# Taps loaded as rows and turned on TensorE, the routing token turned earlier, and the first norm's epsilon and mean handled by GpSimd

## The chip, the cores and the metric

The kernel runs on one core of a Trainium2 chip. The metric is the device time in microseconds of one execution. Engines are named as in the profile: PE is TensorE, PEld its loads of the stationary operand, DVE VectorE, ACT ScalarE, POOL GpSimd, SP the engine that issues most DMAs.

## The reference

One pre-norm block on x of shape (8, 1024, 256), all float32:

```
x = x + mixer(layernorm(x));  x = x + experts(layernorm(x))
layernorm: (x - mean) / sqrt(var + 1e-5), over the 256 features
mixer: xp, z = split(x @ w_in)                     # 256 -> 512 + 512
       xc = silu(causal_conv(xp, conv_w) + conv_b) # 4 taps per channel, depthwise
       h[t] = 0.9 h[t-1] + 0.1 (xc[t] @ w_B)       # 512 -> 16
       y = (h @ w_C) * silu(z);  return y @ w_out  # 512 -> 256
experts: scores = x[:, 0, :] @ Wr + br             # first token of each sequence
       top 2 of 8; mean over them of gelu(x @ W1[e] + b1[e]) @ W2[e] + b2[e]
```

## The kernel before

The 8192 tokens are worked in 16 chunks of 512 (TT = 4 tiles of 128 tokens), two chunks a sequence. Chunk a is in the mixer, chunk a - 1 in the output projection and second norm, chunk a - 2 in the experts, all in one step. The first three chunks are written out by hand in `opening()` of every engine, one more step follows, then a hardware loop and a written-out end. Each engine has its own program (sync, gpsimd, scalar, vector, tensor blocks) and runs it strictly in order; semaphores with counts tie them together. There is no planner: the order in each `opening()` and `step()` is the schedule.

Every product is made of three TensorE passes over operands split into a high and a low part (`_hi`, `_lo`): hi by hi, lo by hi, hi by lo. ScalarE casts the high part; VectorE or GpSimd subtracts it from the value for the low part. Normed tokens must be turned (tokens on partitions to features on partitions); for chunks 0 to 3 TensorE does it (`turns`), later the data go through DRAM and VectorE.

What the change touches:
- Opening loads. SP issues the first half of chunk 0, `w_in` in three parts, chunk 1, eight copies of `w_C`, `w_out` and the rest. ScalarE's queue carries the second half of chunk 0, the taps `tap_w` (L583, runs of 16 bytes), `tap_b` (L585, 4 bytes each) and `wb_raw` (L586).
- First norm of chunk 0 in halves of two tiles. VectorE makes the moments (`stats1_first`: L883, L888), the negated mean (L892) and variance plus epsilon (L893); GpSimd the power -1/2 (L480); VectorE the normed tiles (`norm1_first`, L900). TensorE turns each half (`turns1_first`, L1218) behind WARM = 32 turns of the identity (L1466), ScalarE casts it, and `xp_first` (L1290, L1293, L1301) makes the first products.
- First norm of the other chunks. VectorE: `stats1`, `moments1` (L848, then L851 negates the means and L852 adds epsilon). GpSimd: `pow1` (L395) and `norm1` (L408, adds the negated mean and multiplies).
- Taps. ScalarE does tap 0 with the bias (`first_taps`, L651), VectorE the other three (`tap`, L958), reading one column of `tap_w` per block.
- Second norm and routing of chunk 0. ScalarE: `norm2(0, 0)`, four tiles (L634), then `first_token(0)`, `state_hi(1, 1)`, `gates(2, 2)`. TensorE: `z(2, (0, 1, 2))`, then `turns2_first`: tile 0 (L1241), the token's two turns into `blk[0]` (L1247), the other tiles, `score(0, 0)` (L1459), and `z(2, (3,))`. VectorE: `route(0)` picks the experts, then `state_lo(1, 1)`, a tap, `ys(1, (0,))`, `turn2_lo(0)`. TensorE's `up_first` (L1349, L1353, L1357) starts the experts of chunk 0.

## Time and profile before

| | us |
|---|---|
| median of 3 runs | 510.37 (510.25 to 510.47) |
| the profiled execution, its own time | 510.43 |
| its span in the profile | 508.5 |
| TensorE busy | 503.3 |
| VectorE busy | 453.2 |
| ScalarE busy | 401.0 |
| GpSimd busy | 343.1 |

A timeline row gives the start from the beginning of the span, the time from the first start to the last end of the merged instructions, the engine, the source line, the operation, what is written and read, the count, and in brackets the idle time before it with what ended it. TensorE's instructions are pipelined: each is shown longer than its turn on the array, so the distance between starts is what it costs, and the last of a group ends later than its turn. A row with four products of 512 columns and 1.07 us holds three distances of 0.227 and one product of 0.39.

### The profile page before, as it was taken

Reading aid. Unit: us, or ns where it says so; the run is one execution under the profiler, and the core shown is the slowest. Engines: PE = TensorE matmul, PEld = TensorE weight load, DVE = VectorE, ACT = ScalarE, POOL = GpSimd, SP = SyncE. Lnnn points to the kernel's source line nnn. Section 1 sums busy time; section 2 is a strip of 40 time slices with the busy share of each in tenths; the row PEclk is TensorE's granted clock in tenths of the full one; section 3 lists DMA queues with packets and bytes.
Section 4 is the critical chain, followed back from the end, with each engine's and each line's share of the span. In section 5 each row is a group of like instructions: output and inputs, shape, how many; then the busy total and the mean of one; then the engine's idle time right before and its main releaser. Section 6 shows DMA issues by size and latency. Waiting matters only on the chain.

```text
span 508.5 us, 9829 instructions
## 1 busy us (share of the span) xinstructions
PE 503.3 (99%) x3026; PEld 447.5 (88%) x3026; DVE 453.2 (89%) x900; ACT 401.0 (79%) x694; POOL 343.1 (67%) x384
## 2 busy tenths in 40 slices
PE   8999999999999999999999999999999999999997
PEld 8878799889898989989899998989989899898997
DVE  6999999999998899979999899998999889896773
ACT  4886958888869789697886969879797888969454
POOL 4866587649694696928969197772977649773291
PEclk9999999999999999999999999999999999999999
DMA  8940104435151542606235171542604333130102
GB/s 263 291 177 1 42 1 167 124 125 167 62 175 56 156 132 83 206 0 206 83 124 165 41 217 30 165 124 78 211 31 147 111 124 126 50 116 0 43 2 83
DMA packets 53378, 57.27 MB, mean 113 GB/s; under 512 B 8682, under 2 KB 49642, under 8 KB 53226
## 3 DMA queue, kind: packets, MB, share of 16 engines
q1 hardware_dynamic: 51498, 56.67, 34.8%
q10 hardware_dynamic: 1856, 0.31, 0.3%
q8 instruction: 12, 0.20, 0.2%
q14 instruction: 12, 0.10, 0.1%
HBM read 35.46 MB, written 21.50 MB: 112 GB/s over the span
## 4 chain that ended last, share of the span: by engine, by line
PE 93%; DVE 1%; POOL 0%; issue 0%; DVEq 0%
PE blk L1257 15%; PE blk L1258 15%; PE blk L1262 15%; PE tok L1374 12%; PE tok L1376 12%; PE tok L1375 12%; PE turn L1415 3%; PE turn L1418 3%; PE blk L1437 3%; PE turn L1209 1%; POOL normed L408 0%; PE tok L1262 0%; PE tok L1257 0%; PE tok L1258 0%; PE turn L1258 0%; PE turn L1257 0%
## 5 line engine op out<-in xcount | busy, mean ns | idle before, releaser
L958 DVE SCALAR_TENSOR_TENSOR conv<-blk,tap_w,conv 128x512 f32<-128x512 f32 x192 | 130.1, 742 | 7.8 <-ACT conv L651 7.1
L462 POOL TENSOR_TENSOR y_lo<-gate,y_hi 128x512 fp32r<-128x512 f32 x57 | 72.2, 1297 | 36.6 <-ACT y_hi L580 36.6
L1257 PE MATMUL blk<-xn_hi,w_in_hi 128*128 128x512 f32 x228 | 89.5, 393 | 0.0
L1258 PE MATMUL blk<-xn_hi,w_in_lo 128*128 128x512 f32 x228 | 89.0, 391 | 0.0
L427 POOL TENSOR_TENSOR xc_lo<-conv,xc_hi 128x512 fp32r<-128x512 f32 x59 | 70.9, 1218 | 8.8 <-ACT xc_hi L580 8.0
L1374 PE MATMUL tok<-w_out_hi,y_hi 128*128 128x256 f32 x256 | 72.1, 282 | 0.0
L1376 PE MATMUL tok<-w_out_hi,y_lo 128*128 128x256 f32 x256 | 71.8, 281 | 0.0
L1375 PE MATMUL tok<-w_out_lo,y_hi 128*128 128x256 f32 x256 | 71.8, 281 | 0.0
L1262 PE MATMUL blk<-xn_lo,w_in_hi 128*128 128x512 f32 x228 | 70.3, 389 | 0.0
L1374 PE MATMUL tok<-w_hi,hid_hi 128*128 128x256 f32 x248 | 69.9, 282 | 0.0
L1376 PE MATMUL tok<-w_hi,hid_lo 128*128 128x256 f32 x248 | 69.6, 281 | 0.0
L1375 PE MATMUL tok<-w_lo,hid_hi 128*128 128x256 f32 x248 | 69.5, 280 | 0.0
L651 ACT ACTIVATE conv<-blk,tap_b,tap_w 128x512 f32<-128x512 f32 x64 | 48.9, 777 | 25.0 <-PE blk L1262 22.4
L657 ACT ACTIVATE conv<-conv 128x512 f32<-128x512 f32 x64 | 39.3, 629 | 31.3 <-DVE conv L958 30.3
L829 DVE TENSOR_TENSOR hid_lo<-hid,hid_hi 128x512 fp32r<-128x512 f32 x64 | 45.4, 736 | 17.6 <-ACT hid_hi L580 17.3
L470 POOL TENSOR_TENSOR x_mid<-x_mid,b_sel 128x256 f32<-128x256 f32 x60 | 45.7, 794 | 12.9 <-ACT normed L634 7.9
L1262 PEld LDWEIGHTS blk<-xn_lo,w_in_hi 128*128 128x128 f32 x228 | 42.8, 188 | 9.2
L1258 PEld LDWEIGHTS blk<-xn_hi,w_in_lo 128*128 128x128 f32 x228 | 42.9, 188 | 8.0
L1257 PEld LDWEIGHTS blk<-xn_hi,w_in_hi 128*128 128x128 f32 x228 | 42.8, 188 | 8.0
L1375 PEld LDWEIGHTS tok<-w_out_lo,y_hi 128*128 128x128 f32 x256 | 49.0, 191 | 0.6
L1374 PEld LDWEIGHTS tok<-w_out_hi,y_hi 128*128 128x128 f32 x256 | 48.0, 188 | 0.8
L1375 PEld LDWEIGHTS tok<-w_lo,hid_hi 128*128 128x128 f32 x248 | 47.4, 191 | 1.1
(185 smaller groups left out, 1320.9 us busy)
## 6 DMA issues: line engine op xcount, KB each, us to landing
spill<-normed SPq DMA_DIRECT2D x25, 512.0 KB, 2.8
normed<-spill SPq DMA_DIRECT2D x100, 128.0 KB, 2.9
out<-x_mid SPq DMA_DIRECT2D x30, 256.0 KB, 2.8
x_mid<-in_L_attn_x SPq DMA_DIRECT2D x29, 256.0 KB, 2.8
x_in<-in_L_attn_x SPq DMA_DIRECT2D x14, 512.0 KB, 4.6
w_all<-in_L_ffn_W SPq DMA_DIRECT2D x2, 2048.0 KB, 11.6
b_all<-in_L_ffn_b SPq DMA_DIRECT2D x1, 1024.0 KB, 13.1
gate<-in_L_attn_w_in SPq DMA_DIRECT2D x2, 256.0 KB, 4.7
```

Of the source, the lines that this page charges most:

```text
L427: nc.gpsimd.tensor_tensor(xc_lo[:, j, :], conv[:, j, 0:CH], xc_hi[:, j, :].bitcast(F32), ALU.subtract).then_inc(xc_lo_set, 1)
L462: nc.gpsimd.tensor_tensor(y_lo[:, j, :], gate_of(o, j), y_hi[:, j, :].bitcast(F32), ALU.subtract).then_inc(y_lo_set, 1)
L470: ins = nc.gpsimd.tensor_tensor(mid(f, q)[:, n, :], mid(f, q)[:, n, :], b2_sel[:], ALU.add)
L651: nc.scalar.activation(conv[:, j, HALO:HALO + CH], blk[j][:], ACT.Identity, bias=tap_b[:, j:j + 1], scale=tap_w[:, j, 0:1]).then_inc(tap_f ...
L829: return nc.vector.tensor_tensor(dst, src, hi.bitcast(F32), ALU.subtract)
L958: nc.vector.scalar_tensor_tensor(cols, blk[j][:], tap_w[:, j, t:t + 1], cols, ALU.mult, ALU.add).then_inc(tap_added, 1)
L1257: mm(dst, whi(k), his(k), start=(k == 0), stop=False)
L1258: mm(dst, wlo(k), his(k), start=False, stop=False)
L1262: ins = mm(dst, whi(k), los(k), start=False, stop=(k == KD - 1))
L1374: mm(dst, his[:, j, rows], whi, start=(j == 0 and n == 0), stop=False, skip_group_check=True)
L1375: mm(dst, his[:, j, rows], wlo, start=False, stop=False, skip_group_check=True)
L1376: ins = mm(dst, los[:, j, rows], whi, start=False, stop=(last and n == 1), skip_group_check=True)
```

## The change

The convolution's taps and bias are loaded as rows: channel block j on partition j, 2 KB and 512 bytes contiguous. Behind the 26th of the 32 warm-up turns TensorE waits for them and turns each tap and the bias (five turns of 4 by 128) into a bank; VectorE copies the 20 columns to `taps_all`. `wb_raw` moves from ScalarE's queue to SP's, ahead of the copies of `w_C`.

The first norm no longer has a negated mean: the mean is subtracted. In chunk 0 the fourth tile is centred and scaled by ScalarE between its casts of `w_in` instead of by VectorE, TensorE waiting for it before that tile's turn and GpSimd before its first low part. In the other chunks VectorE only makes the moments; GpSimd adds epsilon, waits for itself, and takes the power.

The routing token is turned on TensorE behind `z(2, (0, 1))`, in front of `z(2, (2,))`; ScalarE casts it between the second and third tile of `norm2(0, 0)`; the score is issued behind tile 1 instead of behind tile 3; `gates(2, 2)` goes ahead of `state_hi(1, 1)`.

```diff
@@ -46,8 +46,9 @@
-        tap_w = sb("tap_w", [P, JD, TAPS])
-        tap_b = sb("tap_b", [P, JD])
+        taps_all = sb("taps_all", [P, TAPS + 1, JD])
+        tap_b = taps_all[:, TAPS, :]
+        tap_rows = sb("tap_rows", [JD, (TAPS + 1) * P])
         w_router, w_spread = sb("w_router", [P, KD, E]), sb("w_spread", [P, KD, E])
@@ -289,6 +292,7 @@
                 sp.dma_start(x_mid[:, 1, half_rows(h), :], x_t[1][:, half_rows(h), :]).then_inc(res_loaded[1][h], 16)
+            sp.dma_start(wb_raw[:], w_B.rearrange("(j p) s -> p j s", p=P)).then_inc(mix_loaded, 16)
             for r in range(P // NST):
@@ -392,6 +396,10 @@
                 pool.wait_ge(stats1_ready, c + 1)
+                pool.sem_inc(passed, 1)
+                nc.gpsimd.tensor_scalar(var_eps1[:], mean_var1[:, :, 1], EPS, None, ALU.add).then_inc(eps_added, 1)
+                pool.wait_ge(eps_added, c)
+                pool.sem_inc(passed, 1)
                 nc.gpsimd.tensor_tensor(rstd1[:], var_eps1[:], minus_half[:], ALU.pow).then_inc(rstd1_set, 1)
@@ -405,7 +413,7 @@
                         dst, src = by_group(normed1, n), src.rearrange("p (k g j) -> p k g j", k=KD, g=QUADS)
-                    ins = nc.gpsimd.tensor_scalar(dst, src, neg_mean[:, n:n + 1], rstd1[:, n:n + 1], ALU.add, ALU.mult)
+                    ins = nc.gpsimd.tensor_scalar(dst, src, mean_var1[:, n, 0:1], rstd1[:, n:n + 1], ALU.subtract, ALU.mult)
                 ins.then_inc(norm1_ready, 1)
@@ -480,6 +488,7 @@
                 pool.wait_ge(norm1_ready, 1)
+                pool.wait_ge(tile_normed, 1)
                 for part in (1, 2):
@@ -580,10 +589,8 @@
             act.dma_start(x_mid[:, 0, half_rows(1), :], x_t[0][:, half_rows(1), :]).then_inc(res_loaded[0][1], 16)
-            act.dma_start(tap_w[:], conv_w.rearrange("(j p) o t -> p j (o t)", p=P)).then_inc(taps_loaded, 16)
-            with nc.allow_non_contiguous_dma(reason="a small transposed load, once"):
-                act.dma_start(tap_b[:], conv_b.rearrange("(j p) -> p j", p=P)).then_inc(taps_loaded, 16)
-            act.dma_start(wb_raw[:], w_B.rearrange("(j p) s -> p j s", p=P)).then_inc(mix_loaded, 16)
+            act.dma_start(tap_rows[:, 0:TAPS * P], conv_w.rearrange("(j p) o t -> j (p o t)", p=P)).then_inc(taps_loaded, 16)
+            act.dma_start(tap_rows[:, TAPS * P:], conv_b.rearrange("(j p) -> j p", p=P)).then_inc(taps_loaded, 16)
             act.wait_ge(consts_set, 1)
@@ -609,6 +616,19 @@
+            def centre_tile():
+                act.wait_ge(stats1_ready, 1)
+                hi(neg_mean[:], mean_var1[:, TT - 1, 0:1], -1.0).then_inc(mean_negated, 1)
+                act.wait_ge(mean_negated, 1)
+                nc.scalar.activation(by_token(normed1, TT - 1), tokens_in(0)[:, TT - 1, :], ACT.Identity,
+                                     bias=neg_mean[:]).then_inc(tile_centred, 1)
+
+            def scale_tile():
+                act.wait_ge(tile_centred, 1)
+                act.wait_ge(rstd1_set, 1)
+                nc.scalar.activation(by_token(normed1, TT - 1), by_token(normed1, TT - 1), ACT.Copy,
+                                     scale=rstd1[:, TT - 1:TT]).then_inc(tile_normed, 1)
+
             def turn1_hi_first(h):
@@ -709,11 +729,13 @@
                 in_hi(0)
+                centre_tile()
                 in_hi(1)
+                scale_tile()
                 turn1_hi_first(0)
...
                 in_hi(2)
-                act.wait_ge(taps_loaded, 32)
+                act.wait_ge(taps_set, 1)
                 first_taps(0, (0, 1))
@@ -758,10 +780,11 @@
                 gates(2, 0)
-                norm2(0, 0)
+                norm2(0, 0, (0, 1))
                 first_token(0)
+                norm2(0, 0, (2, 3))
+                gates(2, 2)
                 state_hi(1, 1)
-                gates(2, 2)
                 gates(2, 1)
@@ -842,14 +865,13 @@
                 dve.wait_ge(norm1_ready, c)
-                dve.wait_ge(stat1_step, c * 2 + 3)
+                if isinstance(c, int) and c == 1:
+                    dve.wait_ge(tile_normed, 1)
+                dve.wait_ge(stat1_step, c + 4)
                 dve.sem_inc(passed, 1)
...
                     ins = nc.vector.bn_aggr(mean_var1[:, n, :], stats1_t[:, n, :])
-                ins.then_inc(stat1_step, 1)
-                dve.wait_ge(stat1_step, c * 2 + 4)
-                nc.vector.tensor_scalar(neg_mean[:], mean_var1[:, :, 0], -1.0, None, ALU.mult)
-                nc.vector.tensor_scalar(var_eps1[:], mean_var1[:, :, 1], EPS, None, ALU.add).then_inc(stats1_ready, 1)
+                ins.then_inc(stats1_ready, 1)
@@ -889,16 +911,15 @@
                 cols = half_rows(h)
-                nc.vector.tensor_scalar(neg_mean[:, cols], mean_var1[:, cols, 0], -1.0, None, ALU.mult)
                 nc.vector.tensor_scalar(var_eps1[:, cols], mean_var1[:, cols, 1], EPS, None,
...
                 dve.sem_inc(passed, 1)
-                for n in (2 * h, 2 * h + 1):
-                    ins = nc.vector.tensor_scalar(by_token(normed1, n), tokens_in(0)[:, n, :], neg_mean[:, n:n + 1],
-                                                  rstd1[:, n:n + 1], ALU.add, ALU.mult)
+                for n in (2 * h, 2 * h + 1)[:2 - h]:
+                    ins = nc.vector.tensor_scalar(by_token(normed1, n), tokens_in(0)[:, n, :], mean_var1[:, n, 0:1],
+                                                  rstd1[:, n:n + 1], ALU.subtract, ALU.mult)
                 ins.then_inc(norm1_ready if h else half_normed, 1)
@@ -1047,9 +1068,12 @@
                 in_lo_first(1)
+                dve.wait_ge(taps_turned, 1)
+                nc.vector.tensor_copy(taps_all[:].rearrange("p t j -> p (t j)"),
+                                      tok[1][:, 0:(TAPS + 1) * JD]).then_inc(taps_set, 1)
                 turn1_lo_first(0)
                 turn1_lo_first(1)
-                dve.wait_ge(taps_loaded, 32)
+                dve.wait_ge(taps_set, 1)
                 edge(0, True)
@@ -1210,11 +1234,21 @@
+            def turn_taps():
+                pe.wait_ge(taps_loaded, 32)
+                by_tap = tap_rows[:, 0:TAPS * P].rearrange("j (p t) -> j t p", t=TAPS)
+                for t in range(TAPS + 1):
+                    src = by_tap[:, t, :] if t < TAPS else tap_rows[:, TAPS * P:]
+                    ins = nc.tensor.transpose(tok[1][:, t * JD:(t + 1) * JD], src, ident[0:JD, 0:JD])
+                ins.then_inc(taps_turned, 1)
+
             def turns1_first():
...
                         for t in (2 * h, 2 * h + 1):
+                            if t == TT - 1 and k == 0:
+                                pe.wait_ge(tile_normed, 1)
                             ins = nc.tensor.transpose(half_bank(h, k)[:, t * P:(t + 1) * P],
@@ -1231,10 +1265,16 @@
+            def token_first():
+                pe.wait_ge(tap_added, last_tap(2, 0))
+                pe.wait_ge(norm2_ready, 1)
+                for k in range(KD):
+                    nc.tensor.transpose(blk[0][:, k * P:(k + 1) * P], by_token(normed2, 0)[:, k * P:(k + 1) * P],
+                                        ident[:]).then_inc(token_turned, 1)
+
             def turns2_first():
...
                 pe.wait_ge(gate_set, 2 * JD + 1)
-                pe.wait_ge(tap_added, last_tap(2, 0))
                 for t in range(TT):
@@ -1242,11 +1282,8 @@
                             ins.then_inc(turned2, 1)
-                    if t == 0:
-                        for k in range(KD):
-                            nc.tensor.transpose(blk[0][:, k * P:(k + 1) * P], by_token(normed2, 0)[:, k * P:(k + 1) * P],
-                                                ident[:]).then_inc(token_turned, 1)
-                score(0, 0)
+                    if t == 1:
+                        score(0, 0)
@@ -1462,7 +1499,9 @@
                 pe.wait_ge(consts_set, 3)
-                for _ in range(WARM):
+                for n in range(WARM):
+                    if n == WARM - 6:
+                        turn_taps()
                     nc.tensor.transpose(tok[0][:, 0:P], ident[:], ident[:])
@@ -1489,7 +1528,9 @@
                 state_in(1)
-                z(2, (0, 1, 2))
+                z(2, (0, 1))
+                token_first()
+                z(2, (2,))
                 turns2_first()
```

## Rows read from the trace of the kernel before

**Rows 1.** The page's busy times over the whole span.
```profile
PE 503.3 (99%) x3026; PEld 447.5 (88%) x3026; DVE 453.2 (89%) x900; ACT 401.0 (79%) x694; POOL 343.1 (67%) x384
```

**Rows 2.** TensorE's waits from 8 us on: total us, times, longest.
```profile
PE tok L1257 <- ACT gate L669: 0.5, 1, 0.5
PE turn L1209 <- POOL normed L408: 0.3, 1, 0.3
```

**Rows 3.** Windows: stretch, its length, busy us (x instructions) by engine, clock, DMA, GB/s.
```profile
60.00:500.00 440.00, 440.00 (x2673) 392.75 (x2673) 396.82 (x768) 354.55 (x608) 303.58 (x336) 1.00 0.33 107
```

**Rows 4.** TensorE's timeline, opening: start, us, line, out<-in, count, [idle before].
```profile
1.84 5.33 PE L1466 MATMUL tok<-ident 128*128 128x128 f32 x24
...
7.17 0.88 PE L1466 MATMUL tok<-ident 128*128 128x128 f32 x6
...
7.88 0.60 PE L1218 MATMUL blk<-ident,normed 128*128 128x128 f32 x4
8.58 0.66 PE L1218 MATMUL turn<-ident,normed 128*128 128x128 f32 x4
```

**Rows 5.** DMA issues: queue, count, KB each, us from issue to landing.
```profile
x_mid<-in_L_attn_x ACTq DMA_DIRECT2D x1, 256.0 KB, 3.6
...
tap_b<-in_L_attn_conv_b ACTq DMA_DIRECT2D x1, 2.0 KB, 6.8
```

**Rows 6.** VectorE's timeline, 6 to 25 us.
```profile
6.67 0.74 DVE L900 TENSOR_SCALAR normed<-x_mid,neg_mean,rstd 128x256 f32<-128x256 f32 x2
...
7.79 0.74 DVE L900 TENSOR_SCALAR normed<-x_mid,neg_mean,rstd 128x256 f32<-128x256 f32 x2
...
12.25 0.91 DVE L851 TENSOR_SCALAR neg_mean<-mean_var 128x4 f32<-128x4 f32 x1
...
13.15 6.67 DVE L958 SCALAR_TENSOR_TENSOR conv<-blk,tap_w,conv 128x512 f32<-128x512 f32 x10
...
24.51 0.17 DVE L851 TENSOR_SCALAR neg_mean<-mean_var 128x4 f32<-128x4 f32 x1
```

**Rows 7.** ScalarE's timeline, 6 to 13 us.
```profile
6.95 0.63 ACT L580 ACTIVATE w_in_hi<-gate 128x512 fp32r<-128x512 f32 x1 [0.79 <-DMA gate<-in_L_attn_w_in]
...
8.30 0.66 ACT L580 ACTIVATE xn_hi<-blk 128x256 fp32r<-128x256 f32 x2 [0.72 <-PE blk L1218]
...
11.75 1.45 ACT L651 ACTIVATE conv<-blk,tap_b,tap_w 128x512 f32<-128x512 f32 x2 [1.09 <-PE blk L1301]
```

**Rows 8.** GpSimd's timeline, 10 to 52 us.
```profile
10.73 2.41 POOL L474 TENSOR_TENSOR w_in_lo<-gate,w_in_hi 128x1024 fp32r<-128x1024 f32 x1 [0.73 <-ACT w_in_hi L580]
...
24.83 1.46 POOL L395 TENSOR_TENSOR rstd<-var_eps,minus_half 128x4 f32<-128x4 f32 x1 [1.81 <-DVE var_eps L852]
26.49 2.16 POOL L408 TENSOR_SCALAR normed<-x_in,neg_mean,rstd 128x256 f32<-128x256 f32 x4 [0.20 <-issue]
...
51.08 0.20 POOL L422 TENSOR_TENSOR shift<-neg_mean,rstd 128x4 f32<-128x4 f32 x1 [0.18 <-POOL rstd L419]
```

**Rows 9.** TensorE's timeline, 27 to 60 us.
```profile
27.38 1.07 PE L1418 MATMUL tok<-xc_lo,b_mix 128*128 128x512 f32 x4
...
28.71 1.09 PE L1209 MATMUL turn<-ident,normed 128*128 128x128 f32 x8 [0.26 <-POOL normed L408]
...
51.82 0.39 PE L1257 MATMUL tok<-xn_hi,w_in_hi 128*128 128x512 f32 x1
...
54.37 0.24 PE L1459 MATMUL blk<-w_router,first_tok 128*1 128x8 f32 x4
55.12 0.50 PE L1257 MATMUL tok<-xn_hi,w_in_hi 128*128 128x512 f32 x1 [0.50 <-ACT gate L669]
...
58.49 1.49 PE L1353 MATMUL blk<-xn_lo,w_hi 128*128 128x512 f32 x4
```

**Rows 10.** ScalarE's timeline at the second norm of chunk 0.
```profile
51.31 2.09 ACT L634 ACTIVATE normed<-x_mid,shift,rstd 128x256 f32<-128x256 f32 x4
```

**Rows 11.** VectorE's timeline behind the routing.
```profile
57.69 1.28 DVE L829 TENSOR_TENSOR xn_lo<-turn,xn_hi 128x512 fp32r<-128x512 f32 x2
```

More of the change, by code:

```diff
@@ L61, in build_block @@
         rstd1, rstd2 = sb("rstd1", [P, TT]), sb("rstd2", [P, TT])
-        neg_mean = sb("neg_mean", [P, TT])
+        neg_mean = sb("neg_mean", [P, 1])
         neg_mean2, shift2 = sb("neg_mean2", [P, TT]), sb("shift2", [P, TT])
@@ L109, in build_block @@
         wout_loaded = sem("wout_loaded")
[L110 removed]
+        taps_loaded, taps_turned, taps_set = sem("taps_loaded"), sem("taps_turned"), sem("taps_set")
         mix_loaded = sem("mix_loaded")
@@ L977, in edge @@
                 if opens:
-                    src = tap_b[:].rearrange("p (j o) -> p j o", o=1).broadcast_to([P, JD, HALO])
+                    src = tap_b.rearrange("p (j o) -> p j o", o=1).broadcast_to([P, JD, HALO])
                 else:
```

7 lines of the change are left out of this document (4 added, 3 removed).

## The prediction

> **What bounds the kernel now.** I read the page's busy times first: TensorE is busy 99% of the span [rows 1]. Then its waits: in the whole span it waits for other engines twice after its start, 0.3 and 0.5 us [rows 2]. The windows show it busy 440.00 of the 440 us from 60 to 500 [rows 3]. So nothing that the change does in the steady steps can pay; an edit pays only where it closes a hole in TensorE's row before 60 us, and hurts where it opens one or adds TensorE work. The timeline shows four holes. (a) Between the two halves of the first turns: four turns start at 7.88, at 0.11 us a piece they are through at 8.32, and the next four start at 8.58 [rows 4]: 0.26 of idle, and 0.06 more because the first turn behind a pause takes 0.17 instead of 0.11. (b) Before turns1(2) at 28.71: the last of the four products that start at 27.38, 0.227 apart, leaves the array at 28.29, so 0.42 plus 0.06 of restart [rows 9]. (c) Between the score (four steps, the last starting at 54.45) and z(2,3) at 55.12, 0.64 and 0.11 of restart. (d) Inside L1353: four products take 1.49, where four together take 1.07 (0.39 for the last, 0.227 for the others): 0.42 [rows 9]. Together 1.97 us, 0.39% of the time: about the most that can be won.
>
> **The opening: what it removes.** Each half of the first statistics drops one neg_mean operation on VectorE, about 0.08 of its time (two such operations of 0.17 overlap in the 0.32 between 24.51 and the pow at 24.83 [rows 6, 8]); the second half's var_eps is thus 0.16 sooner. norm1_first(1) norms one tile instead of two: it began at 7.79 and took 0.74 for two [rows 6], so it now ends near 8.00 (7.79 - 0.16 + 0.38). The other tile is ScalarE's: negate (about 0.2), centre (0.38, half of a 512-wide copy's 0.63 [rows 7] with its fixed part) from about 6.65, then in_hi(1), which started at 6.95 and now waits till about 7.3, takes 0.63, then scale 0.38: ready at about 8.3. The second half's turns could start at 8.1 instead of 8.58.
>
> **The opening: what it adds.** TensorE works in order, and the 32 warm-up turns, not the data, set the first turns: 24 of them run from 1.84 for 5.33, 0.213 a piece, the six from 7.17 take 0.88, 0.11 a piece but for the first (the clock rises from 1.2 to 2.4 GHz there), and the first half's normed tiles are ready at 7.41 (6.67 + 0.74), before 7.88 [rows 4, 6]. The five tap turns are inserted behind the 26th, at 7.17. No row shows a turn with a 128-column stationary operand and 4 moving columns. Lower bound 0.025 (the score's steps, 0.24 for four with 0.17 for the last, one stationary column [rows 9]): 0.13 in all. Upper bound: full turns at the low clock, 0.213: 1.07. Nearest is a full turn at 2.4 GHz, 0.11, with the same stationary operand but 32 times the moving columns; I take 0.08, 0.40 in all. First turns then start at 8.28, the second four follow at once at 8.72 (tiles ready at 8.3), and are through at 9.16, where they were at 9.07 (8.58 + 0.17 + three of 0.11): hole (a) of 0.31 is used up and **+0.1** is left (bounds -0.2 and +0.8). ScalarE's first cast follows the turns (it began at 8.30 behind 7.88 [rows 7]), so it begins at about 8.7 and ends at 9.08, just before TensorE wants it; the second operand is wanted at 9.4 and there at 9.36. This cover is thin: 0.05.
> The Trainium skill (TensorE: Matmul & The Clock Gate, LDWEIGHTS) says that a weight load costs by its columns and not by its rows, so that loading 4 rows by 128 columns costs what 128 by 128 does; by its formula, an estimate, 0.107 a load, 0.53 for five, and the sum below would end at 509.9. No row here separates the load from the moving part.
>
> The loads: taps as rows are 4 runs of 2 KB and 4 of 512 B, where 512 and 512 tiny ones went. tap_b landed 6.8 us after its issue at about 1.8, the 256 KB of x_mid ahead of it on the same queue 3.6 after its issue at 0.7 [rows 5]. So the new ones land after 4.3 and, if they cost no more than the old, by 8.6. I take 5: TensorE reaches them at 7.17, so they are hidden by 2 us. wb_raw goes behind six issues on SP's queue; every later issue (eight of w_C, w_out, x_in, the router, the experts' weights) is about 0.5 later. Their first reader is ScalarE after 13.1, at the end of the two products' taps that begin at 11.75 [rows 7]; a delay of a few tenths there meets taps that VectorE reaches only at 16.5. Cost 0, up to 0.1.
>
> **VectorE and the first hole in the steps.** L851 at 12.25 took 0.91 and ended with GpSimd's L474 (10.73 plus 2.41 is 13.14), where one of its size takes 0.17 [rows 6, 8]: it was held by GpSimd. It goes, and VectorE's first tap, 13.15 before, waits only for ScalarE's first taps, 11.75 plus 0.78, and the second for 13.2. From the third tap on VectorE is about 0.6 ahead; with the opening's 0.1, 0.5. The new copy of the taps out of PSUM, 0.17, falls at 8.5 to 8.7 before a wait for ScalarE. If GpSimd holds it as it held L851, it ends near 9.7, and the 0.5 is lost.
> moments1(2) loses two operations: the moments were done at 24.51, where the first of them starts, and the pow started at 24.83 [rows 6, 8], of which I take 0.25 as won. GpSimd adds epsilon: a small operation of 0.20 and 0.18 of waiting for its own result, as before L422 [rows 8]. So its pow starts 0.5 + 0.25 - 0.38 = 0.37 earlier than 24.83, and the four norm tiles, 26.49 to 28.66, end at 28.3, or sooner if the pow's 1.46 [rows 8] was stretched by VectorE's work beside it. TensorE arrives at 28.29 + 0.1. Hole (b) closes: **-0.48**. If VectorE's 0.5 is lost, GpSimd is 0.13 late and the hole grows by 0.1: bounds -0.48 and +0.1.
> What comes after moves with TensorE: turn casts, scan, gates, y_lo are released by it or by VectorE, which has gained as much.
>
> **The routing token.** ScalarE's four norm2 tiles start at 51.31, 0.50 apart and 0.6 long [rows 10], so tile 0 is ready at 51.95; TensorE ends z(2,1) at 51.82 [rows 9]: the token's turns wait, 0.13 plus 0.06. z(2,2) then runs from 52.25 to 53.6, with the token's two one-column casts at 52.45, two tiles of norm2 behind it until 53.65. Turns of tiles 0 and 1, then the score's last step at 54.23, where it was at 54.45. Tiles 2 and 3 turn by 54.7, the gate that z(2,3) wants (gates(2,2), now ahead of state_hi) is done at 54.35: z(2,3) starts at 54.7 instead of 55.12, hole (c) closed but for the new 0.2. Yet that is not what comes last: VectorE's route, state_lo, tap and turn2_lo follow the score. turn2_lo(0), 57.69 and 1.28 long [rows 11], releases the second product of L1353. This chain moves by 0.22, so of (c) 0.22 is kept and TensorE waits longer in (d) and for state_lo. **-0.22** (bounds 0 and -0.45). w1 is cast 0.1 to 0.16 sooner, and GpSimd's w_lo behind it is due 0.5 later.
>
> **Steady steps.** GpSimd gets 0.38 more in each of 13 chunks, VectorE loses 0.16 to 1.0. TensorE never waits there [rows 3]: 0.
>
> **The sum**: +0.1 - 0.48 - 0.22 = -0.6. Against the profiled execution (span 508.5, 1.93 around it, 510.43) 509.83; that is 0.06 above the median of the runs, so 509.77.
>
> **Rivals.** (1) The opening eats it: the tap turns run near the low clock's 0.213 each, or the copy is held by GpSimd. Then +0.5 to +0.8, hole (b) closes partly, route kept: +0.6 - 0.48 - 0.22 = -0.1, 510.27. For it: they start at the very turn of the clock. Against: the row of six. (2) More: tap turns at 0.03, so -0.2, and the route's chain shorter, -0.45: 509.25. For it: the score's steps; against: turn2_lo is a fixed chain. (3) Slower: the wait on the tap load stands in front of the last warm-up turns, and in front of the first half of the tokens. If the load lands after 7.17, TensorE stands and every tenth is paid in full; at the old landing of tap_b, 8.6, that is +1.4, and if the clock, whose rise at 7.2 came after 5.6 us of unbroken turns, stays at 1.2 GHz through as long again, half of it, 2.8, comes on top. It decides from a landing at 7.17; net of the other -0.6 that is +0.8 (511.2) without the clock and +3.6 (514.0) with it; I name the middle, 512.6. Against: the load lies behind only 256 KB that landed at 4.3. (4) The change does not do what it says, the old holes reopening one engine further on: 510.4.
> In a sentence of its own: the Trainium skill (TensorE: Matmul & The Clock Gate, Part 4: PE-mode transpose) says that transposes do not count as work that lifts the clock; here the rise came behind 26 of them and nothing else [rows 4], so this trace disagrees, and inserted turns should neither help nor hinder it.
>
> **Chances.** Forecast 0.56 (509.77, its own range 509.4 to 510.1); (1) 0.16; (2) 0.10; (3) 0.08; (4) 0.10. 0.2%, 1.02 us, is about what a measurement can tell from no change. Faster by more (under 509.35) is (2) and a corner of the forecast: 0.13. Slower (over 511.39) is (3): 0.07. The rest 0.80. Range 509.1 to 510.8: it takes in (1), (4) and most of (2), and leaves out (3).
>
> **What would show it.** Tap turns: five short TensorE rows at 7.17, and the first turns about 0.4 after 7.88; no pause between the two halves. L851 gone and the first VectorE tap near 12.6. No TensorE wait on GpSimd's normed near 28. The score near 0.2 sooner relative to turns1(2), no wait for a gate, but waits on state_mix and xn_lo. TensorE's span from there to the end unchanged behind L1353 (508.5 - 58.5 = 450.0). A tap load landing after 7.2, or a TensorE wait in the steady steps, would make the forecast wrong.

## The result, and the profile after

The changed kernel takes 532.63 us (median of 4 runs, 528.16 to 535.02) against 510.34 for the kernel before in the same comparison: 1.0427 times as long, interval 1.0400 to 1.0454. The prediction was 509.77. The profiled execution took 533.95, span 532.0.

The page's busy times (as [rows 1]) show TensorE busy 10.1 us longer and the span longer by 23.5, so 13.4 of it is new idle time. The 10.1 are no new work: about 5 are three stretches at the lower of TensorE's two clocks (1.7 us each, see the end), and the rest, an estimate from the distances between its starts, is delays too short for the page to show as idle. GpSimd is busy 52.7 us more and VectorE 20.1:

```profile
PE 513.4 (96%) x3031; PEld 450.6 (85%) x3031; DVE 473.3 (89%) x868; ACT 404.7 (76%) x697; POOL 395.8 (74%) x399
```

The costliest groups after: line, engine, operation, busy time and mean ns.

```profile
L416 POOL TENSOR_SCALAR normed<-x_in,mean_var,rstd 128x256 f32<-128x256 f32 x56 | 67.9, 1225 | 2.8 <-POOL rstd L403 2.0
...
L852 DVE TENSOR_TENSOR xn_lo<-normed,xn_hi 128x512 fp32r<-128x512 f32 x50 | 65.8, 1356 | 1.4 <-ACT xn_hi L589 0.7
```

GpSimd's norm tile, the line that only swapped `add` of the negated mean for `subtract` of the mean, takes 1225 ns; four of the old ones together took 2.16 in [rows 8]. Sixty tiles (56 here, four of chunk 1) by 0.67 are 40 of GpSimd's 52.7. The group of VectorE's low parts of the normed tiles has grown too, by 21.8, though the change doesn't touch it. This is how the same group stood before:

```profile
L829 DVE TENSOR_TENSOR xn_lo<-normed,xn_hi 128x512 fp32r<-128x512 f32 x50 | 44.0, 919 | 1.4 <-ACT xn_hi L580 0.7
```

TensorE's waits after (as [rows 2]; the wait for ident is its start, as before):

```profile
PE turn L1455 <- POOL xc_lo L435: 4.6, 3, 2.0
PE blk L1299 <- DVE xn_lo L852: 4.4, 4, 2.5
PE turn L1233 <- POOL normed L416: 2.2, 1, 2.2
PE tok L1411 <- DVE hid_lo L852: 1.7, 3, 0.6
PE tok L1505 <- POOL ident L393: 1.6, 1, 1.6
PE blk L1474 <- DVE state_mix L852: 0.7, 3, 0.3
PE blk L1394 <- POOL w_lo L445: 0.3, 1, 0.3
```

Behind the start 7.1 us of them are waits for GpSimd and 6.8 waits for VectorE's low parts.

The windows (as [rows 3]) show the two places where the time goes, the opening, and the steady steps, where TensorE had been busy 440.00 of 440:

```profile
12.00:20.00 8.00, 6.15 (x30) 4.85 (x28) 7.36 (x15) 6.64 (x14) 7.53 (x7) 1.00 0.71 184
20.00:28.00 8.00, 7.63 (x31) 6.27 (x32) 5.51 (x15) 6.03 (x11) 7.58 (x11) 0.79 1.08 383
...
60.00:500.00 440.00, 427.98 (x2531) 375.80 (x2530) 406.53 (x717) 347.00 (x593) 338.22 (x334) 0.99 0.33 106
```

GpSimd's timeline of the opening gives the first of them, chunk 1's norm; the row below it is that norm in the kernel before:

```profile
13.80 0.24 POOL L400 TENSOR_SCALAR var_eps<-mean_var 128x4 f32<-128x4 f32 x1
14.23 1.04 POOL L403 TENSOR_TENSOR rstd<-var_eps,minus_half 128x4 f32<-128x4 f32 x1 [0.18 <-POOL var_eps L400]
15.48 4.84 POOL L416 TENSOR_SCALAR normed<-x_mid,mean_var,rstd 128x256 f32<-128x256 f32 x4 [0.21 <-issue]
```

```profile
14.54 2.17 POOL L408 TENSOR_SCALAR normed<-x_mid,neg_mean,rstd 128x256 f32<-128x256 f32 x4 [0.22 <-issue]
```

It takes 4.84 for four tiles, and TensorE, which turned them at 17.41 before, stands until 20.37. Behind that pause the granted clock is 0.79 of full in 20 to 28 us: products of 512 columns then start 0.43 apart until 24.7; they start 0.23 apart before the pause and again from 25. TensorE's timeline:

```profile
17.54 0.61 PE L1299 MATMUL tok<-xn_lo,w_in_hi 128*128 128x512 f32 x2
20.37 1.09 PE L1233 MATMUL turn<-ident,normed 128*128 128x128 f32 x8 [2.22 <-POOL normed L416]
...
22.12 0.63 PE L1294 MATMUL tok<-xn_hi,w_in_hi 128*128 128x512 f32 x1
22.54 0.63 PE L1295 MATMUL tok<-xn_hi,w_in_lo 128*128 128x512 f32 x1
```

In the steady steps the largest single loss is a VectorE low part. Its timeline and GpSimd's, at 159 to 167 us:

```profile
159.31 1.28 DVE L881 TENSOR_TENSOR x_mid<-tok,x_mid 128x512 f32<-128x512 f32 x2
160.62 7.24 DVE L852 TENSOR_TENSOR xn_lo<-normed,xn_hi 128x512 fp32r<-128x512 f32 x2
...
159.31 2.36 POOL L435 TENSOR_TENSOR xc_lo<-conv,xc_hi 128x512 fp32r<-128x512 f32 x2
161.61 2.83 POOL L478 TENSOR_TENSOR x_mid<-x_mid,b_sel 128x256 f32<-128x256 f32 x4
164.40 2.31 POOL L435 TENSOR_TENSOR xc_lo<-conv,xc_hi 128x512 fp32r<-128x512 f32 x2
```

Two low parts take 7.24 where they take 1.3 undisturbed; the first alone has 6.64. GpSimd runs without a break to 166.71, and the first low part ends 0.55 behind that: it was held while GpSimd's train (its operations one behind the other, without a pause) passed, and then did its own work. TensorE waits 2.5 us for it, and again the clock falls, to a mean of 0.57 in the 4 us behind the wait:

```profile
168.00:172.00 4.00, 4.00 (x11) 3.13 (x12) 3.67 (x19) 2.13 (x4) 1.23 (x2) 0.57 0.00 0
```

### The profile page after: what moved, and what is told of

Same layout as the page of the kernel before. It is cut to its first block, busy times and chain, and to the rows that moved or that the text cites. A ratio compares the mean times of both kernels' runs of the same rounds, so it can differ in the third digit from the quotient of the medians.

```text
span 532.0 us, 9853 instructions
## 1 busy us (share of the span) xinstructions
PE 513.4 (96%) x3031; PEld 450.6 (85%) x3031; DVE 473.3 (89%) x868; ACT 404.7 (76%) x697; POOL 395.8 (74%) x399
## 4 chain that ended last, share of the span: by engine, by line
PE 62%; DVE 10%; POOL 10%; issue 8%; ACT 3%; ACTq 1%; DVEq 0%; POOLq 0%
PE blk L1294 10%; PE blk L1299 10%; PE blk L1295 9%; PE tok L1411 8%; PE tok L1413 8%; PE tok L1412 8%; POOL xc_lo L435 3%; PE blk L1474 3%; DVE xn_lo L852 2%; DVE conv L979 2%; POOL w_lo L445 2%; POOL normed L416 2%; PE turn L1455 2%; DVE hid_lo L852 2%; PE turn L1452 2%
## 5 line engine op out<-in xcount | busy, mean ns | idle before, releaser
L979 DVE SCALAR_TENSOR_TENSOR conv<-blk,taps_all,conv 128x512 f32<-128x512 f32 x192 | 130.2, 741 | 8.9 <-ACT conv L671 7.8
L435 POOL TENSOR_TENSOR xc_lo<-conv,xc_hi 128x512 fp32r<-128x512 f32 x59 | 73.2, 1257 | 5.6 <-ACT xc_hi L589 5.5
L1411 PE MATMUL tok<-w_hi,hid_hi 128*128 128x256 f32 x248 | 71.0, 286 | 1.7 <-DVE hid_lo L852 1.7
L416 POOL TENSOR_SCALAR normed<-x_in,mean_var,rstd 128x256 f32<-128x256 f32 x56 | 67.9, 1225 | 2.8 <-POOL rstd L403 2.0
L671 ACT ACTIVATE conv<-blk,taps_all 128x512 f32<-128x512 f32 x64 | 49.4, 778 | 26.9 <-PE blk L1299 24.5
L852 DVE TENSOR_TENSOR xn_lo<-normed,xn_hi 128x512 fp32r<-128x512 f32 x50 | 65.8, 1356 | 1.4 <-ACT xn_hi L589 0.7
L852 DVE TENSOR_TENSOR hid_lo<-hid,hid_hi 128x512 fp32r<-128x512 f32 x64 | 47.9, 786 | 11.2 <-ACT hid_hi L589 10.8
L478 POOL TENSOR_TENSOR x_mid<-x_mid,b_sel 128x256 f32<-128x256 f32 x60 | 51.4, 887 | 4.8 <-DVE hid_lo L852 4.1
L716 ACT ACTIVATE hid<-blk,b_sel 128x512 f32<-128x512 f32 x64 | 43.3, 677 | 11.2 <-PE blk L1299 9.0
L1411 PEld LDWEIGHTS tok<-w_hi,hid_hi 128*128 128x128 f32 x248 | 47.4, 191 | 4.0 <-DVE hid_lo L852 3.0
```

What stands on the lines that cost most here:

```text
L416: ins = nc.gpsimd.tensor_scalar(dst, src, mean_var1[:, n, 0:1], rstd1[:, n:n + 1], ALU.subtract, ALU.mult)
L435: nc.gpsimd.tensor_tensor(xc_lo[:, j, :], conv[:, j, 0:CH], xc_hi[:, j, :].bitcast(F32), ALU.subtract).then_inc(xc_lo_set, 1)
L478: ins = nc.gpsimd.tensor_tensor(mid(f, q)[:, n, :], mid(f, q)[:, n, :], b2_sel[:], ALU.add)
L852: return nc.vector.tensor_tensor(dst, src, hi.bitcast(F32), ALU.subtract)
L979: nc.vector.scalar_tensor_tensor(cols, blk[j][:], taps_all[:, t, j:j + 1], cols, ALU.mult, ALU.add).then_inc(tap_added, 1)
L1411: mm(dst, his[:, j, rows], whi, start=(j == 0 and n == 0), stop=False, skip_group_check=True)
```

## The experiments

Two theories stood at first. A: GpSimd's `subtract, mult` form is itself slow. B: the tile is slow because of its operands or of what runs beside it.

**e1.** Seven forms of GpSimd's 128x256 operation on one core with nothing beside them, six of each; the rest of the block is left out.

```diff
+    forms = [(ALU.add, ALU.mult), (ALU.subtract, ALU.mult), (ALU.mult, ALU.add), (ALU.mult, ALU.subtract),
+             (ALU.add, None), (ALU.subtract, None), (ALU.mult, None)]
```

> A kernel that leaves the whole block out and only runs GpSimd tensor_scalar on one 128x256 tile, six times in each of seven forms of its two operations. Theory A (the operation: GpSimd is slow at subtract followed by mult): the form subtract, mult takes about 1.22 us as in the changed kernel, add, mult 0.556 as in the one before, the others tell whether subtract or its place is slow. Theory B (the operand: a mean read with a step of two, or VectorE beside it): all forms take about 0.55 us here.

The groups, in the order resb `subtract, mult`, resd `mult, subtract`, rese to resg one operation alone (add, mult, subtract, each 924), resc `mult, add`, resa `add, mult`:

```profile
L57 POOL TENSOR_SCALAR resb<-src,mv 128x256 f32<-128x256 f32 x6 | 7.3, 1223 | 0.6
L57 POOL TENSOR_SCALAR resd<-src,mv 128x256 f32<-128x256 f32 x6 | 7.3, 1222 | 0.6
...
L55 POOL TENSOR_SCALAR resg<-src,mv 128x256 f32<-128x256 f32 x6 | 5.5, 924 | 0.6
...
L57 POOL TENSOR_SCALAR resc<-src,mv 128x256 f32<-128x256 f32 x6 | 3.3, 557 | 0.6
L57 POOL TENSOR_SCALAR resa<-src,mv 128x256 f32<-128x256 f32 x6 | 3.3, 554 | 2.7 <-DMA src<-in_L_attn_x 2.2
```

A is shown: two scalars with add and mult in either order take 0.555; one subtract among them makes it 1.22, and a single operation, add too, takes 0.92, more than two. B falls.

**e2.** The kernel before with that form alone.

```diff
-ins = nc.gpsimd.tensor_scalar(dst, src, neg_mean[:, n:n + 1], rstd1[:, n:n + 1], ALU.add, ALU.mult)
+ins = nc.gpsimd.tensor_scalar(dst, src, mean_var1[:, n, 0:1], rstd1[:, n:n + 1], ALU.subtract, ALU.mult)
```

> The kernel before with one line changed: GpSimd's norm1 subtracts the mean from mean_var1 instead of adding neg_mean; everything else stays, the negated mean is still made. If that line is the cause of the loss (theory A or B), 60 tiles go from 0.556 to 1.22 us and the time is 528 to 535. Rival C (the cause is GpSimd's added epsilon and its wait, or the new chunk-0 code): the time stays at 510.3.

544.66 (542.27 to 548.89), ratio 1.0678 (1.0618 to 1.0738): the form alone costs more than the whole change, and more than I expected. Its main waits were VectorE's:

```profile
PE blk L1262 <- DVE xn_lo L829: 10.7, 10, 2.0
PE tok L1374 <- DVE hid_lo L829: 7.5, 6, 1.7
PE turn L1209 <- POOL normed L408: 3.8, 2, 1.9
```

Ten of its low parts are held for 2.8 to 6.1 us; in the changed kernel it is four, for 3.3 to 6.6.

**e3.** The changed kernel with `add` for `subtract`; it computes x plus the mean.

```diff
-ins = nc.gpsimd.tensor_scalar(dst, src, mean_var1[:, n, 0:1], rstd1[:, n:n + 1], ALU.subtract, ALU.mult)
+ins = nc.gpsimd.tensor_scalar(dst, src, mean_var1[:, n, 0:1], rstd1[:, n:n + 1], ALU.add, ALU.mult)
```

> The changed kernel with add in the place of subtract in GpSimd's norm1, the operand still mean_var1 (it computes x + mean, so it leaves the right value out). Theory A (operation): 0.556 a tile, TensorE without waits in the steady steps, 509.5 to 510.3. Theory B (operand with step two): 1.22 a tile, 528 to 535 as the changed kernel.

509.94 (509.33 to 510.66), ratio 0.9988 (0.9978 to 0.9997); after its start TensorE waits once, 0.4. The tile takes 0.555 though it reads the same operand. One word in one line carries all of the 22 us, and everything else of the change together brings 0.5 (before took 510.42 in this comparison), which is what the prediction said of it (0.6).

**e4.** The repair that keeps VectorE out: GpSimd negates the mean itself in one more small operation and uses `add, mult`.

```diff
+nc.gpsimd.tensor_scalar(neg_means[:], mean_var1[:, :, 0], -1.0, None, ALU.mult).then_inc(eps_added, 1)
...
-ins = nc.gpsimd.tensor_scalar(dst, src, mean_var1[:, n, 0:1], rstd1[:, n:n + 1], ALU.subtract, ALU.mult)
+ins = nc.gpsimd.tensor_scalar(dst, src, neg_means[:, n:n + 1], rstd1[:, n:n + 1], ALU.add, ALU.mult)
```

> The changed kernel with a negated mean made by GpSimd (one more operation of 0.23 us on 128x4 per chunk) and add, mult in norm1. Theory A and B: 0.556 a tile again, steady steps without TensorE waits, and the time is what the rest of the change is worth: 509.8 by the old sum with the measured tap turns put in (five steps of 0.12 instead of 0.08, so +0.2 more: 510.0). If a part of the loss lies elsewhere, it stays above 511.

515.78 (515.00 to 516.29), ratio 1.0100 (1.0084 to 1.0117): my expectation missed by 5.8. The fast form is back, and 0.2 more a chunk on GpSimd than in e3 still costs 5.8 us. TensorE waits nowhere longer than 0.2; the time is in the distances between its starts. Behind the five held low parts ten of them are 0.17 to 0.38 longer than usual, 2.8 together, and six at `state_mix` are 0.2 to 0.3 longer, 1.5 together. VectorE's low parts take 1304 on the mean, five of them 4.2. GpSimd and VectorE at one of the five:

```profile
214.57 2.83 POOL L480 TENSOR_TENSOR x_mid<-x_mid,b_sel 128x256 f32<-128x256 f32 x4
217.35 2.34 POOL L437 TENSOR_TENSOR xc_lo<-conv,xc_hi 128x512 fp32r<-128x512 f32 x2
...
214.77 1.27 DVE L883 TENSOR_TENSOR x_mid<-tok,x_mid 128x512 f32<-128x512 f32 x2
216.07 4.77 DVE L854 TENSOR_TENSOR xn_lo<-normed,xn_hi 128x512 fp32r<-128x512 f32 x2
```

The first low part (4.17) starts inside the four adds and ends 0.55 behind the last of two later GpSimd operations, at 219.69. So a second loss exists that needs no slow form, only a shifted meeting of the two engines.

**e5.** How long is it held? A VectorE operation of 128x512, started 0.4 into a train of four GpSimd operations, each pairing three times (`tt` is two tensors, `tt_gaps` the same with a wait behind each, `tt_psum` one VectorE operand in PSUM, `tt_scalar` one tensor and two scalars); the block is left out.

```diff
+    phases = ["none", "tt", "add_mult", "sub_mult", "tt_gaps", "tt_psum", "tt_scalar"] * 3
```

> A kernel that leaves the whole block out. VectorE starts one 128x512 operation about 0.4 us into a train of four back-to-back GpSimd operations of the same width; seven phases, three times each. Theory H (a VectorE operation that reads two SBUF operands, or runs in its fast one-operand mode, is held until the GpSimd train leaves a pause): two SBUF operands beside four tensor_tensor (1.27 each) take 4 to 5 us, beside add, mult and subtract, mult as long as those trains, with a pause of 0.2 between the GpSimd operations about 1 to 1.5; with one operand in PSUM 0.65; without a train 0.65. Rival S (both only share the port and slow each other): never more than about twice 0.65, and the pauses change little.

VectorE alone, then beside a train of two-input operations, and GpSimd's train:

```profile
7.24 0.69 DVE L92 TENSOR_TENSOR vc<-va,vb 128x512 f32<-128x512 f32 x1
...
8.50 1.42 DVE L92 TENSOR_TENSOR vc<-va,vb 128x512 f32<-128x512 f32 x1
```

```profile
8.11 1.26 POOL L74 TENSOR_TENSOR gca<-ga,gb 128x512 f32<-128x512 f32 x1 [7.28 <-DVE vc L92]
9.33 1.71 POOL L74 TENSOR_TENSOR gcb<-ga,gb 128x512 f32<-128x512 f32 x1
```

It is held to the end of the operation that runs (9.37) and takes 0.55 from there; GpSimd's next then waits in turn, 1.71 instead of 1.26. With one operand in PSUM it takes 0.69, not held. With one SBUF operand and two scalars it takes 1.12 and GpSimd's next operation 1.44, held as well; that form wasn't run alone. With gaps between GpSimd's operations it takes 1.49. The theory of a held train fails here: the hold is one operation long.
The Trainium skill (SBUF — State Buffer, SBUF: two separate sides) says that a VectorE instruction with two inputs in SBUF and a GpSimd instruction that reads SBUF exclude each other from a shared pair of ports, each for its full instruction. This run agrees; the 4.17 and 6.64 us of the kernels are longer than one instruction and do not.

**e6.** e4 with a wait for itself behind each of GpSimd's 128x256 adds and low parts, so that its train has gaps of 0.08 to 0.16.

```diff
+                    if not isinstance(a, int) or a > 3:
+                        pool.wait_ge(xc_lo_set, a * JD + j + 1)
...
-                ins.then_inc(b2_added, 1)
+                    nc.gpsimd.tensor_tensor(mid(f, q)[:, n, :], mid(f, q)[:, n, :], b2_sel[:],
+                                            ALU.add).then_inc(b2_added, 1)
+                    pool.wait_ge(b2_added, f * TT + n + 1)
```

> The variant with GpSimd's negated mean (515.8 us), and a wait added behind each of GpSimd's four b2 additions and each convolution low part in the looped steps, so that it pauses about 0.2 us between them: GpSimd gets 1.4 us more to do per chunk. Theory H: VectorE's xn_lo, 4.2 us long when four such operations follow one another, slips in, its mean falls from 1.30 to under 1.0, and the time falls by 3 to 6 us, to 510 to 512. Rival G (GpSimd is simply late): the time rises above 516.

512.01 (511.65 to 512.15), ratio 1.0029 (1.0017 to 1.0041), 3.8 less than e4 though GpSimd does the same work and pauses besides. The same place as in e4 now takes 2.15 for two, and no low part takes over 1.6:

```profile
213.63 3.86 POOL L482 TENSOR_TENSOR x_mid<-x_mid,b_sel 128x256 f32<-128x256 f32 x4
217.65 1.09 POOL L437 TENSOR_TENSOR xc_lo<-conv,xc_hi 128x512 fp32r<-128x512 f32 x1 [0.16 <-POOL x_mid L482]
...
214.74 2.15 DVE L857 TENSOR_TENSOR xn_lo<-normed,xn_hi 128x512 fp32r<-128x512 f32 x2
```

In the kernel, then, a low part is held long only where the train is unbroken. Yet an unbroken train doesn't always hold it. In the changed kernel the same order stands again at 228.85, with the low part started 0.07 into the same operation of the train (0.06 at 160.62) and 27 ns behind VectorE's add (31); there the first low part takes 1.57, one operation's hold, where it took 6.64:

```profile
228.85 2.72 DVE L852 TENSOR_TENSOR xn_lo<-normed,xn_hi 128x512 fp32r<-128x512 f32 x2
```

**e7.** The changed kernel with GpSimd's part alone undone: VectorE negates the mean and adds epsilon as before, and GpSimd's norm adds the negated mean.

```diff
-nc.gpsimd.tensor_scalar(var_eps1[:], mean_var1[:, :, 1], EPS, None, ALU.add).then_inc(eps_added, 1)
+nc.vector.tensor_scalar(neg_means[:], mean_var1[:, :, 0], -1.0, None, ALU.mult)
+nc.vector.tensor_scalar(var_eps1[:], mean_var1[:, :, 1], EPS, None, ALU.add).then_inc(stats1_ready, 1)
...
-ins = nc.gpsimd.tensor_scalar(dst, src, mean_var1[:, n, 0:1], rstd1[:, n:n + 1], ALU.subtract, ALU.mult)
+ins = nc.gpsimd.tensor_scalar(dst, src, neg_means[:, n:n + 1], rstd1[:, n:n + 1], ALU.add, ALU.mult)
```

> The changed kernel with its GpSimd part undone: VectorE makes the negated mean and var_eps of chunks 1 to 15 again, GpSimd only the power and add, mult. The opening (tap turns, fourth tile on ScalarE) and the routing token stay. If all the loss is in GpSimd's part: 509.6 to 510.2 (opening +0.6 by the trace, hole before turns1(2) -0.5, token -0.2 to -0.3). If placing or timing matters elsewhere, up to 515.

510.20 (509.94 to 510.87), ratio 0.9998 (0.9988 to 1.0007). The tap rows, ScalarE's tile and the token's order come to nothing together; the low parts are back at 918, and TensorE has no wait behind its start.

**e8.** The kernel before with the token's new order alone.

```diff
-                z(2, (0, 1, 2))
+                z(2, (0, 1))
+                token_first()
+                z(2, (2,))
```

> The kernel before with the routing token's part alone. By the prediction -0.22 (bounds 0 and -0.45): 510.1 to 510.2; TensorE no longer waits for the gate before z(2,3), but for state_mix or the low part of the turned tokens.

510.56 (510.31 to 511.32), ratio 1.0004 (0.9995 to 1.0013). The step did what it says and gained nothing. VectorE and GpSimd behind the score, and the two operations that meet as they stood in the kernel before:

```profile
54.53 0.15 DVE L1035 TENSOR_TENSOR scores<-blk,b_router 1x8 f32<-1x8 f32 x1 [0.32 <-PE blk L1463]
...
55.39 0.97 DVE L830 TENSOR_TENSOR state_mix<-state,state_mix 64x512 fp32r<-64x512 f32 x1
...
54.51 1.30 POOL L427 TENSOR_TENSOR xc_lo<-conv,xc_hi 128x512 fp32r<-128x512 f32 x1
```

```profile
55.58 0.81 DVE L829 TENSOR_TENSOR state_mix<-state,state_mix 64x512 fp32r<-64x512 f32 x1
...
54.57 1.27 POOL L427 TENSOR_TENSOR xc_lo<-conv,xc_hi 128x512 fp32r<-128x512 f32 x1
```

The scores come 0.20 sooner (54.73 before). But `state_mix`, 0.81 long from 55.58 before, now takes 0.97 from 55.39. It ends 0.55 behind the end of GpSimd's `xc_lo` in both kernels: at 56.39 behind 55.84 before, at 56.36 behind 55.81 now. GpSimd's operation had hardly moved, so the gain ends there.

**e9.** The changed kernel with e6's pauses: how much of the 22 us is held low parts?

> The changed kernel, subtract kept, with the pauses of 0.15 to 0.2 us behind each b2 addition and convolution low part in the looped steps. Theory H (the longer norm pushes GpSimd's trains onto VectorE's splits, which are held until a train ends): xn_lo's mean falls from 1.36 towards 1.0, the time from 532 to 516 to 526 although GpSimd has 1 us more to do per chunk. Theory L (GpSimd is too long as such: 2.66 us more per chunk reach TensorE directly, by xc_lo and normed): 532 or more.

525.49 (524.83 to 527.10), ratio 1.0303 (1.0287 to 1.0320): 7 of 22 go with the holds (low parts 1174 on the mean instead of 1356). What TensorE still waits for behind its start is GpSimd itself, 12.1 in all:

```profile
PE turn L1458 <- POOL xc_lo L435: 8.7, 6, 2.0
PE turn L1236 <- POOL normed L416: 3.1, 2, 2.2
```

**e10.** The kernel before with three of the four tiles normed twice by the fast form, the second time into a spare tile: the extra time (1.67 a chunk) without a subtract.

```diff
+if n < 3:
+    nc.gpsimd.tensor_scalar(spare[:, n, :], tokens_in(c)[:, n, :], neg_mean[:, n:n + 1],
+                            rstd1[:, n:n + 1], ALU.add, ALU.mult)
```

> The kernel before, whose GpSimd norm writes three of the four tiles a second time into a spare tile, by the fast add, mult: 1.67 us more per chunk instead of subtract's 2.66, no subtract anywhere. If only GpSimd's length and timing count, the loss is of subtract's kind: 516 to 535, with VectorE's xn_lo held longer. If the loss needs subtract itself (its way of using the port), the time stays within 1 us of 510.4.

530.75 (530.20 to 530.97), ratio 1.0400 (1.0384 to 1.0416), low parts 1546 on the mean with five of 5.0 to 5.1: a fast form repeated costs nearly as much as the change, so the loss needs nothing of the slow form but its time. For 1.67 instead of 2.66 more a chunk it costs 20 instead of e2's 34: 0.81 and 0.86 of GpSimd's added time (15 chunks: 25 and 40). That is no fixed price: the changed kernel with 3.1 more a chunk, 46 in all, loses 22, under half. How GpSimd's and VectorE's operations meet counts beside the length.

**e11.** e7 with five warm-up turns fewer, as many as there are tap turns.

```diff
-                for n in range(WARM):
+                for n in range(WARM - 5):
```

> The changed kernel with the statistics on VectorE (510.2 us), and five of the six warm-up turns behind the tap turns left out. The tiles of the first half are ready at 7.1 and of the second at 8.1, the last warm-up turn ends near 8.76 there. If the added tap turns are what ate the opening's gain, the first turns start 0.5 earlier and the time falls to 509.6 to 509.9. If the clock or the casts hold instead, it stays at 510.2.

510.03 (509.83 to 510.33), ratio 0.9992 (0.9983 to 1.0001). The first turns start at 7.49 instead of 8.66 in the changed kernel and 7.98 in e7, but the second four wait for their tile until 8.28, as in hole (a). It has the lowest time of the versions that compute the reference, and isn't clearly faster than before.

**e12.** e11 with GpSimd adding epsilon and VectorE negating.

```diff
+nc.gpsimd.tensor_scalar(var_eps1[:], mean_var1[:, :, 1], EPS, None, ALU.add).then_inc(eps_added, 1)
-nc.vector.tensor_scalar(var_eps1[:], mean_var1[:, :, 1], EPS, None, ALU.add).then_inc(stats1_ready, 1)
```

> The changed kernel with VectorE making the negated mean, GpSimd adding epsilon (add, mult in the norm), and five warm-up turns fewer. By the sums: opening +0.1, the hole before turns1(2) about -0.3, token 0: 509.9 to 510.2, unless GpSimd's 0.4 us per chunk brings its trains onto VectorE's splits as the negated mean on GpSimd did (515.8).

511.59 (511.21 to 512.03), ratio 1.0022 (1.0013 to 1.0031): epsilon on GpSimd, 0.4 with its wait, costs 1.6 against e11. Low parts take 1073 on the mean, and hole (b) is back: 0.6 of waiting for `normed`. In e3 the same epsilon on GpSimd lost nothing (509.94); there VectorE makes no negated mean and all 32 warm-up turns stand. Which of the two makes the difference was not run.

**e13 to e15.** Why is a low part held for a whole train in the kernels and for one operation in e5? These three run the kernel's own train by itself (s is a 128x256 add in place, w a 128x512 low part), with the low part in the kernel's operand order, the block left out. A phase of e13 gives train, operand order, statistics ahead and low parts. In e13 VectorE's low part stands behind statistics (b), in e14 also behind an add of PSUM and SBUF (p of 256, q of 512 columns), in e15 with a wait in between that is already met. A dot is a wait of GpSimd for itself.

```diff
+    phases = [("", "squares", 1, 1), ("wwww", "squares", 1, 1), ("ssssww", "squares", 1, 1), ("ssssww", "squares", 1, 2),
+              ("s.s.s.s.w.w", "squares", 1, 2), ("ssssww", "plain", 1, 1), ("ssssww", "squares", 2, 1),
...
+    phases = [("", "q"), ("ssssww", "b"), ("ssssww", "p"), ("ssssww", "q"), ("ssssww", "bq"), ("ssssww", "bbq"),
...
+                if wait:
+                    dve.wait_ge(ready, 4)
```

> The block is left out; only single phases are run, each twice: GpSimd starts a train of operations (s = 128x256 added in place, w = 128x512 low part, as L480 and L437 of the changed kernel), VectorE one or two low parts of 128x512 with both operands in SBUF, the first operand in the squares' order as L852 has it or plain, behind one to three small statistics. Theory (the whole train holds VectorE, and the 128x256 in-place operations or the squares' order make it so, which e5 did not have): 3.5 to 5 us for an operation that falls into ssssww, at most 1.6 with pauses in the train. Rival (an operation is held to the end of GpSimd's operation that runs, and no longer): at most 1.6 us in every phase, with or without pauses; then the 4 to 5 us of the kernels need something more than these two trains. Alone: 0.69 plain, 0.7 to 0.9 in the squares' order.

> The block is left out; single phases, each twice. As e13, but the small VectorE operations ahead of the low part are now statistics (b), or adds of PSUM and SBUF in place (p of 128x256, q of 128x512, as L881 of the changed kernel). In the four traces with holds of 2.3 to 6.6 us every one of them came 25 to 34 ns behind such an add, and no low part behind another operation was held for more than 1.8. Theory (the add in front, directly followed by the low part, lets GpSimd's train keep the way): with p or q in front of the low part beside a train 2.5 to 5 us in at least some of the phases, with b alone at most 1.6, with pauses in the train at most 1.6. Rival (the add in front is a coincidence of the kernels' order): at most 1.6 us in every phase.

> The block is left out; single phases. As e14, but in half of the phases a wait that is already met stands between VectorE's add and the low part, as in the kernels, where the low part starts 25 to 34 ns behind the add (in e14 it overlapped it by 83). Theory (this gap gives GpSimd's train the way): with the wait 2 to 5 us in at least some phases beside ssssww and wwww, without it at most 1.6, with pauses in the train at most 1.6. Rival (neither the order nor the gap does it, something else that the kernels do at that time does): at most 1.6 us everywhere.

The longest low part was 1.54 in e13, 1.25 in e14 and 1.25 in e15. Each rival was right each time; e15 didn't try what it meant to, since the met wait left no gap between the two operations (they still overlap by 83 ns). Neither the add in front nor the gap behind it is enough in the kernels either: in the profile of the changed kernel twelve low parts stand behind that add, all with a gap of 26 to 32 ns, and only four of them are held for more than one operation. What keeps GpSimd's train closed to VectorE in the kernels stays open.

## Why the prediction was wrong

- **The step that failed** is "Steady steps. GpSimd gets 0.38 more in each of 13 chunks ... TensorE never waits there [rows 3]: 0". Its first term was mis-sized: the new form of the norm tile was priced at nothing, so 0.38 a chunk stood for 0.38 + 4 x 0.67 = 3.1 (e1, e3). The same nothing stands in the working of hole (b), where the four norm tiles keep their 2.16. No row of before had a `subtract` beside a scalar `mult` on GpSimd, so the edit needed bounds from both sides, and I gave it none. On VectorE the same change of form was free (two tiles of chunk 0 take 0.73, before 0.74 in [rows 6]). Its second term, the zero, came out for the 0.38 by itself (e3), but with no margin: 0.4 a chunk costs 1.6 in e12, 0.6 a chunk 5.4 in e4. That TensorE is busy 440 of 440 us says that nothing is late; it doesn't say by how much. GpSimd at 67% of the span [rows 1] looked free, but its operations stand between those of VectorE at 89%, and VectorE's are held by them.
- **Hole (b)** closes as worked out where the tile is fast: in e3 the turns start 0.23 behind the last product, -0.48. With VectorE making the statistics (e7) 0.22 of it is left. With GpSimd's longer tile the changed kernel has 0.2 there, but waits 2.2 one chunk earlier, at turns1(1), which no part of the prediction looked at.
- **The opening** cost +0.59 by the first full product (12.52 instead of 11.94), not +0.1, inside the bounds of -0.2 and +0.8. The larger part of the miss is the tap turns' 0.08: TensorE's timeline after has them 0.12 to 0.15 apart, and 0.14 more ahead of the first.

```profile
7.31 0.70 PE L1242 MATMUL tok<-ident,tap_rows 4*128 4x4 f32 x5
7.94 0.87 PE L1505 MATMUL tok<-ident 128*128 128x128 f32 x6
8.65 0.60 PE L1252 MATMUL blk<-ident,normed 128*128 128x128 f32 x4
9.09 0.60 PE L1252 MATMUL turn<-ident,normed 128*128 128x128 f32 x4
```

  0.77 in all, where I had 0.40; the two halves do follow each other without a pause. The other 0.12 lies in the first four products, 0.59 from the last turn's start to the fourth product's instead of 0.46, and why is open.
  A turn of 4 rows steps 0.12 where one of 128 rows steps 0.11. The Trainium skill (TensorE: Matmul & The Clock Gate, LDWEIGHTS) lets a weight load cost by its columns and not by its rows; the trace agrees with that, though it doesn't part the load from the moving columns.
- **The loads** were right: no wait on the tap rows, and wb_raw on its new queue was nobody's wait. So rival (3), the slower one, had the sign and neither the place nor the price: the clock did fall and cost time, but behind a wait for GpSimd at 20 us.
- **The copy out of PSUM** took 0.17 at 8.14, as the forecast had it, but it started 0.09 ahead of GpSimd's low part, so this row doesn't test whether it could be held; in e5 an operation with one operand in PSUM was not held.
- **The token**: -0.22 was 0 (e8). The score moved by 0.20 as worked out; the chain behind it has `state_mix`, and that is tied to GpSimd's `xc_lo`, not to the score. I had seen L851 held in the same way and didn't ask it of the other two-operand operations on the path.
- The rest of the sum came out within 0.2 (e3: 509.94), in part by luck: TensorE's clock rises at 6.3 us in e3's profile, at 7.2 in that of before, behind 7.0 in that of the changed kernel and at 4.2 in e2's, without an edit that reaches it, and e3's first full product starts at 12.11. Where the clock rises in a run moves the opening by more than most of the steps that I priced there.
- **The error** is 22.9, and 22.7 of it is the one line (532.63 against 509.94 in e3). Not all of that falls in the steady steps: at the score of chunk 0 the changed kernel is 4.7 behind e3 (58.62 against 53.92), by the norms of chunks 1 and 2, and 19 more are lost behind it (spans of 532.0 and 508.2).

## What to carry to other kernels

Price an operation by its exact pair of operations, not by its name and size: on GpSimd `add, mult` and `subtract, mult` over 128x256 take 0.555 and 1.22, and where no row shows the new form, that edit needs its own bounds and its count (60). A kernel whose bounding engine never waits may still have no slack behind it; test what 0.4 us more a step on the side engine would do before calling it free. Where two engines exclude each other, read the end of each held operation: if it ends a fixed time behind the other engine's, no earlier start upstream will pay.
